# A causal attention block with a Fourier branch: float32r scores in array halves, and one static order with the stages beside the attention

## The reference

```
xn = layernorm(x)
q, k, v = xn @ wq, xn @ wk, xn @ wv        # q: 16 heads of 16, k and v: 4 heads of 16
q, k = rope(q), rope(k)
scores = einsum('bshd,bthd->bhst', q, k) / 4, causal mask
out = softmax(scores) @ v
y = real(ifft(einsum('bnd,do->bno', fft(xn), w))) + bias     # linear in xn: one 256 x 256 matrix
return x + out @ wo + y
```

## Time and profile before

| What | us |
|---|---|
| Median of 3 runs (1131.06 to 1132.2) | 1131.33 |
| Span of the profiled execution | 1130.0 |
| Busy PE, DVE, ACT, POOL | 1002.3, 866.3, 692.1, 184.0 |
| Opening and projections of batch 0 (0 to 121) | 121 |
| Attention of batch 0 (121 to 548) | 427 |
| Output block of batch 0, projections of batch 1 (548 to 693) | 145 |
| Attention of batch 1 (693 to 1100) | 407 |
| Output block of batch 1 | 30 |

### The profile page before, as it was taken

The page is one execution under the profiler, slowest core; times in us unless marked ns, Lnnn a source line. Parts: engine busy times, 40 slices in busy tenths (PEclk is TensorE's granted clock), DMA queues, the critical chain, the costliest instruction groups (busy, mean ns, idle before and its releaser), DMA issues. The chain is left out here.

```text
span 1130.0 us, 22198 instructions
## 1 busy us (share of the span) xinstructions
PE 1002.3 (89%) x6352; PEld 410.2 (36%) x6352; DVE 866.3 (77%) x1503; ACT 692.1 (61%) x1375; POOL 184.0 (16%) x241
## 2 busy tenths in 40 slices
PE   4975499999999999999888737999999999999998
PEld 3652233333333333322556423333333333333227
DVE  6796388889898888882449836888988988888706
ACT  1451256667677777779525413666767777777882
POOL 4680021010000000000028501211100000000000
PEclk9995699999999999999989758999999999999999
DMA  7099900000000000000014994000000000000002
GB/s 218 19 148 141 124 3 1 2 1 2 1 2 1 1 2 1 2 1 2 31 48 71 144 162 54 2 2 1 1 1 2 1 1 2 1 1 2 1 1 75
DMA packets 44527, 36.01 MB, mean 32 GB/s; under 512 B 11024, under 2 KB 44432, under 8 KB 44432
## 3 DMA queue, kind: packets, MB, share of 16 engines
q1 hardware_dynamic: 44432, 34.74, 17.8%
HBM read 21.89 MB, written 12.58 MB: 31 GB/s over the span
## 5 line engine op out<-in xcount | busy, mean ns | idle before, releaser
L456 ACT ACTIVATE share<-psS 128x512 f32<-128x512 f32 (+2 forms) x1104 | 568.5, 578 | 245.5 <-PE psS L858 240.2
L637 DVE TENSOR_REDUCE pmax<-psA 128x2 f32<-128x1024 f32 x384 | 456.4, 1220 | 54.2 <-PE psA L794 52.4
L794 PE MATMUL psA<-k_st,q_st 96*128 96x512 bf16 (+3 forms) x1280 | 354.5, 360 | 35.5 <-DVE pmax L625 14.7
L858 PE MATMUL psS<-q_st,k_st 98*128 98x512 bf16 (+3 forms) x1232 | 349.8, 350 | 35.3 <-DMA q_st<-spartT 34.0
L831 PE MATMUL psO<-share,v_sb 128*32 128x512 f32 (+3 forms) x2560 | 300.0, 541 | 6.3 <-ACT share L456 3.8
L371 POOL TENSOR_SCALAR_AFFINE_SELECT share<-share 128x512 f32<-128x512 f32 x128 | 81.2, 634 | 828.2 <-ACT share L456 828.2
L858 PEld LDWEIGHTS psS<-q_st,k_st 98*128 98x128 bf16 x1232 | 113.8, 97 | 265.7 <-ACT share L456 142.0
L794 PEld LDWEIGHTS psA<-k_st,q_st 96*128 96x128 bf16 x1280 | 110.3, 100 | 239.5 <-DVE pmax L637 77.4
L633 DVE CUSTOM_DVE_ANT_0 psA<-psA,mask 128x128 f32<-128x128 f32 (+3 forms) x256 | 119.0, 516 | 20.9 <-PE psA L794 20.9
L625 DVE TENSOR_REDUCE pmax<-psA 128x4 f32<-128x512 f32 (+2 forms) x96 | 98.9, 1042 | 22.8 <-PE psA L797 22.5
L831 PEld LDWEIGHTS psO<-share,v_sb 128*32 128x32 f32 x2560 | 50.4, 108 | 108.2 <-ACT share L456 55.3
(11 more groups left out here) (84 smaller groups left out, 631.4 us busy)
## 6 DMA issues: line engine op xcount, KB each, us to landing
q_st<-parts_scratch SPq DMA_DIRECT2D x48, 256.0 KB, 8.8
parts_scratch<-share SPq DMA_DIRECT2D x8, 1024.0 KB, 11.8
x_sb<-in_L_attn_x SPq DMA_DIRECT2D x8, 512.0 KB, 8.2
out<-x_sb SPq DMA_DIRECT2D x8, 512.0 KB, 3.0
k_st<-parts_scratch SPq DMA_DIRECT2D x48, 64.0 KB, 12.4
q_st<-spartT SPq DMA_DIRECT2D x128, 2.0 KB
share<-dft_tables SPq DMA_DIRECT2D x1, 512.0 KB, 4.1
share<-in_L_ffn_w_freq_real SPq DMA_DIRECT2D x1, 256.0 KB, 4.4
```

What stands on the lines that cost most here:

```text
L456: nc.scalar.activation(prob[:, u % 2, k * hp:(k + 1) * hp, s0:CH], score_bank(tail, bank)[:, 0:hp * w].rearrange("p (h s) -> p h s", h=hp) ...
L637: nc.vector.reduce_max(pmax[:, heads[0]:heads[0] + 2, i, q], psA[:, two:two + 2, :], AX.X).then_inc(S["a_reduced"], 1)
L794: last = mm(psA[:, 2 * (v % 2) + k // per, (k % per) * w:(k % per + 1) * w], q_st[0:ROWS, n, r, i * P:(i + 1) * P], k_st[0:ROWS, g, q * CH ...
L858: last = mm(score_bank(tail, bank)[:, h * w:(h + 1) * w], k_st[0:ROWS + SHIFT, g, tile * P:(tile + 1) * P], q_st[0:ROWS + SHIFT, nl, k * h ...
```

## The change

**Numbers.** Queries, keys and the shift are split into two float32r parts instead of three bf16 parts. A stack has 48 rows (three products of parts) and two rows for the shift. Two such stacks lie in one tile, in partitions 0 to 49 and 64 to 113, and hold the query heads r = 0, 1 and r = 2, 3. A score matmul therefore uses 64 rows of the array, and neighbouring matmuls go to opposite halves. The causal mask of the first pass is added on PE for all diagonal uses, by small bf16 matmuls in the same half; L633 is gone. The values product is as before, with 17 instead of 32 columns a head.

**One order.** `schedule()` walks through the whole kernel once when the kernel is built, with a duration for each job on each engine, and picks PE's next job by what is ready. It gives the orders of PE, ACT, POOL, DVE and SP, which are then written out. There is no stage for batch 1 and none for chunks 2 and 3 (chunk 1 is projected in the opening): transposes, projections and output tiles stand between the blocks of attention (`BESIDE` says how many by which step). The scores' ring of three banks is shared with these jobs.

**Rope.** Projections come out transposed, features on partitions, so no parts are transposed. Cosines and sines are spread over 128 partitions in the opening, by PE and ACT. POOL turns 20 of the 24 blocks (six operations of 512 columns each), DVE the first four. Queries are loaded by step (six DMAs for one key head), and kept for eight steps.

**Opening.** x comes in single tiles, statistics are made for four tiles at a time, DVE turns the first blocks, ACT and POOL fill constants and tables, and 30 small matmuls keep PE at work. x of batch 1 lies for its statistics in buffers that are used later.

```diff
-                w = (i + 1) * P if q == n // KV else CH
-                per = len(heads) // 2
...
-                pe.wait_ge(S["a_reduced"], b * ALL + v + 1)
-                for k, r in enumerate(heads):
-                    last = mm(psA[:, 2 * (v % 2) + k // per, (k % per) * w:(k % per + 1) * w], q_st[0:ROWS, n, r, i * P:(i + 1) * P],
-                              k_st[0:ROWS, g, q * CH:q * CH + w], start=True, stop=not on_pe(n, q))
...
+            def a_use(v, o):
...
+                two = slot_free(v)
+                bank = psA[:, two + o, :]
+                lo = (heads[o * per] // 2) * HALF
+                for k in range(per):
+                    last = mm(bank[:, k * w:(k + 1) * w], q_st[lo:lo + ROWS, n % (2 * KV), heads[o * per + k] % 2, i * P:(i + 1) * P],
+                              k_st[lo:lo + ROWS, slot_of(cc - j + q), g, 0:w], start=(k == 0), stop=q != j)
+                if q == j:
+                    for h in range(2):
...
+                        last = mm(to, mask_l[lo:lo + HALF, h, :], mask_r[lo:lo + HALF, h:h + 1, :].broadcast_to([HALF, per, HALF]), start=False, stop=h == 1)
...
+            def scores(g, k):
...
+                if u == 0 and k == 0:
+                    pe.wait_ge(shift_in[n % 2], 32 * CT * (n // 2 + 1))
+                bank = bank_of(("s", g, k))
+                for h in range(hp):
...
+                    lo = (r // 2) * HALF
+                    last = mm(bank[:, h * w:(h + 1) * w], k_st[lo:lo + FULL, key_slot(n, tile), kv, tile % CT * P:(tile % CT + 1) * P],
+                              q_st[lo:lo + FULL, n % (2 * KV), r % 2, s0:CH], start=True, stop=True)
...
+            def load_q(n, t):
...
+                if n >= 2 * KV:
+                    sp.wait_ge(S["pv_done"], BEGIN[n - 2 * KV + 1])
```

More of the change, by code:

```diff
@@ L36, in attention_fourier_block @@
+    STAGE_FIRST = (16, 17, 18, 19, 20)
+    LAG = 2
+    DEEP = 3
+    VW = HD + 1
+    GW = 32
     NEG = -1.0e30
+    WARM = (10, 20)
     EPS = 1e-5
[L38 to L46, removed]
+    QC0, KC0, VC0 = 0, D, D + P
+    WCOLS = D + P + KD
+    BY_HALF = (0, 2, 1, 3)
+    USES = (4, 4, 2, 2)
@@ L79, in attention_fourier_block @@
[L79 to L87, removed]
+        x_sb = sb("x_sb", [P, NJ * CT, D], fp32)
@@ L315, in _, with store @@
-            sp.wait_ge(S["out_stored"], NB * NJ * 16)
+            def store(m):
+                if m in FIRST:
+                    sp.wait_ge(S["first_parts"], 2 * FIRST.index(m) + 2)
+                else:
+                    sp.wait_ge(S["parts_done"], 2 * turned_by_pool(m) + 2)
+                cc = m // 3
+                w = KV if m % 3 == 0 else 2 * KV
+                at = D if m % 3 == 0 else (m % 3 - 1) * P
+                for half in range(2):
+                    for part in range(2):
+                        rows = scratch[cc, part, at:at + w * HD, :].rearrange("(h m n) s -> m h n s", m=2, n=N8)
+                        sp.dma_start(rows[half], parts[half * HALF:half * HALF + w * N8, m % 2, part, :].bitcast(fp32)).then_inc(stored[m % 2], 16)
@@ new lines, in _ @@
+            pool.wait_ge(S["rest_ready"], 5)
+            pool.wait_ge(S["first_parts"], 2 * len(FIRST))
+            before, masks, adds, biases = ("start",), 0, 0, 0
+            for job in POOL_ORDER:
+                if before[0] != "start" and (job[0] == "ones" or (job[0] == "r" and job[2] in (1, 2))):
+                    pool.wait_ge(*done_by(before, masks, adds, biases))
+                if job[0] == "mask":
+                    mask_diag(job[1])
+                    masks += 1
+                elif job[0] == "add":
+                    add_out(job[1], job[2], job[3])
+                    adds += 1
+                elif job[0] == "bias":
+                    add_bias(job[1])
+                    biases += 1
+                elif job[0] == "n":
+                    normalise(job[1])
+                elif job[0] == "ones":
+                    ones_rows(job[1], job[2])
+                else:
+                    rotate(job[1], job[2])
+                before = job
```

1870 lines of the change are left out of this document (1218 added, 652 removed).

## The result

The changed kernel takes 999.38 us (median of 4 runs), the kernel before beside it 1131.76: a ratio of 0.8816, with a 95% interval of 0.879 to 0.8842. The forecast was 845 us, with 812 to 925 as its range. The sign was right, the size was missed by 154 us. The ratio uses three of the four runs; the fourth, at a mean granted clock of 0.93 instead of 0.96 to 0.97, took 1025 us. The profiled run took 994.67 us, of which 993.0 are its span.

The account below looks back on a forecast made before the run. TensorE and VectorE were taken as bounds within 1%: through PE 56 + 742 - 6 + 14 = 806 us, through DVE 801. Waiting of 38 gave 844, and 1.3 carried over gave 845, range 812 to 925.

Parts of the forecast that it names:

- both rivals: Score matmuls: row halves bring no gain, 1015 to 1080 us, chance 0.08; float32r streams at fp32 rate, 1475 us, 0.04.
- changes of mode: TensorE switching between matmul types: 0.09 us each from the earlier trace; some hundred of them for the stages, 9 us.
- Two bf16 loads take 0.31: Stationary loads for score matmuls: two bf16 loads take 0.31 us, one load of 4-byte data 0.195.
- slower than before: Scores at fp32 rate, end 1475 us; slower once a 512-column score costs more than 0.24 us; chance 0.04.
- the bound engine before lost 3 to 5% in attention: Waiting between engines over the whole run: 5% taken, 38 us on 806, giving 844.
- In front of each step DVE is one or more steps ahead: Shift transfers before each attention step: costed at nothing inside the run and at 8 us at the end.
- an exponential that waits on a shift: Sign of being wrong: inside the run, an ACT exponential waiting on a shift transfer.
- No stretch at 1.2 GHz: Sign of being right: no stretch with the clock at 1.2 GHz between the first reduction and the end.
- supply: Late queries, shifts held in SyncE's queue or GpSimd slowing DVE's reductions: 35 to 80 us more, 880 to 925; chance 0.15.
- halves without gain: Score matmuls in opposite row halves save nothing, through waiting loads or taking turns: 1015 to 1080 us; chance 0.08.
- stages apart: Projection and output stages again stand apart from attention: otherwise idle DVE adds 100 us, 945; chance 0.02.

Follow-up runs that it names:

- one-half run: Changed kernel with every score matmul reading the first row half of the array: 1518 us in the median, from 1475 to 1629.
- bf16 runs: Changed kernel with score matmuls reading operands' upper two bytes as bf16, 944 us; and with operands split into two bf16 numbers instead of float32r, 940 us.
- whole, half and eighth work: Changed kernel (998 us) against maxima and exponentials both cut to the first half of their columns (937 us) or the first eighth (916 us).
- TensorE's savings: Changed kernel with values products of half their columns, from 936 to 981 us; and with mask matmuls left out, 991 us.
- an eighth of the work: Changed kernel with each maximum reading and each exponential writing only the first eighth of its columns, copied sums having 1000 added: 916 us.
- dummies: Changed kernel with two dummy fp32 matmuls of 128 columns after each first-pass use before the first second-pass score: 999.5 us.
- two-part bf16 version: Changed kernel with queries, keys and shifts split into two bf16 numbers instead of two float32r ones, order unchanged: 940 us.

## Why the prediction missed, step by step

**What held.** That two halves work at once (0.1175 a matmul against the 0.11 taken), and that float32r does not stream at the fp32 rate: both rivals fell, the first by the one-half run. By its rule that a load overlaps only where the row group differs, the Trainium skill's TensorE: Matmul & The Clock Gate (§ The mechanism) would have made the one-half order pay its loads; it took 0.235 a matmul where a load of 0.19 and 0.235 of columns would make 0.42, so the row holds again. The same section also lets a load go ahead of a matmul in flight into a background weight buffer, which would fit; no run here shows which it is. DVE has 696 us of work from 44.5 us on (731 less 35), 700 in the sum. A whole reduction has a mean of 1.220, as before, and those beside a two-input GpSimd operation (97) 1.221: no contention. Nor did queries run short: TensorE stood for their transfer once, 3.4 us. First reduction 44.9 for 48, last part 13.5 for 14. ACT 653 for 630. DVE was not over 85% busy, though: 74% (663.5 of 897.5 us in the long window), since it stands still for TensorE 110 us ahead of whole reductions alone.

**TensorE's terms.** Scores without changes of mode: 290 (361 less 71), in the sum 302. Values 280, in the sum 309 with 29 for changes of mode, so 280 without. Stages 130 for 122. Changes of mode: 71 (373 stretches of 0.19) for 38. This is the first mis-sized term, +33: the step took bf16's 0.09 from the earlier trace rows for a kind of load that the trace had at 0.195, and counted 320 + 100 changes, but not what the first load costs at each. The bf16 runs show its size. Two slips didn't enter the sum. "Two bf16 loads take 0.31" took the time from the first load's start to the second's end for their cost, where one takes 0.10. And slower than before would have begun at 0.27 us a 512-column score by the forecast's own terms (270 + 325 us over 1792 scores and 768 at half the price), not at 0.24.

**Waiting.** This is the step that failed: "the bound engine before lost 3 to 5% in attention", carried over as 38 us. The score stretches take 160 us over the floor, and at least 80 of it is waiting for DVE and ACT. The percentage came from busy shares, which cover short stops. Yet it was about right for the kernel before: read from starts, its score stretches in batch 1's attention take 262 us, some 20 over 0.09 a stretch and 0.217 for 512 columns (0.17, 0.11 and 0.06 for shorter ones), 5% of 407. The mistake was to carry it over to another balance. Before, DVE and ACT were busy for 328 and 295 us beside TensorE's 393 in batch 1's attention, 83 and 75% of it. Here the step's own sums (700 and about 630 beside 742) made it 94 and 85%, with three score banks and two slots between. That the waiting is for DVE and ACT is shown by the series of whole, half and eighth work; that the closeness of the sums is what made it grow is argued, and fits the 15 and 12 us of TensorE's savings that came back as waiting. The Trainium skill's TensorEngine Tiling (Array Packing) (§ PSUM Bottleneck) says that tiling speeds up TensorE but not the emptying of PSUM, which may then bind; the trace agrees, with 0.52 an exponential against 0.1175 a score matmul.

A smaller part is a term that was put at nothing: "In front of each step DVE is one or more steps ahead". In 14 of the 32 steps the first second-pass score comes only 6 to 10 us after DVE has made the shift (steps 4, 5, 7 to 13, 15 and 28 to 31, counted from 0), and the eight transfers take 5.2 to issue. At step 12 this shows as a stop of ACT:

```profile
362.00 0.21 DVE L1152 STREAM_TRANSPOSE spartT<-spart 128x32 f32<-128x32 f32 x1
...
362.24 5.22 SPq L719 DMA_DIRECT2D q_st<-spartT  x8
...
369.48 1.05 PE L1370 MATMUL psS<-q_st,k_st 50*128 50x512 f32 x3
...
370.20 0.60 ACT L986 ACTIVATE prob_sb<-psS 128x512 f32<-128x512 f32 x1 [10.50 <-PE psS L1370]
```

The stretch around it takes 12.6 us where the floor is 3.5, and with an eighth of the work still 9.9, part of it at 1.2 GHz in both. The prediction named this sign of being wrong, an exponential that waits on a shift. That it is the shift is argued from these times: the order also puts first-pass uses there, and DVE works 11.1 of the 12.6 us. What it cost over the whole run isn't divided from the rest.

**The opening.** First second-pass score at 66.9 for 56, +11: the first step's reductions end at 54.4, with 3 us of waiting for queries, and the order puts a second step's uses ahead of the first second-pass score.

**The clock.** "No stretch at 1.2 GHz" was wrong: 62 us in all (0.031 x 993 x 2), 37.5 of them from 44.4 to 82. They cost at most 31 us, and lie inside the items above, the 160 us over the floor among them.

**The balance.** Forecast span 844, measured 993. From 66.7 to 979.5 us the scores take 502: with the forecast's 6 us of them done earlier, 284 of columns (296 in the sum), 71 of changes of mode (38), 147 over the floor (where 38 of waiting stood). With stages (+8), values (0) and the opening (+11): -12 + 33 + 109 + 8 + 11 = 149. Of the 109, 42 is shown to be waiting (80 less the 38); the other 67 holds low clock, masks dearer than priced and waiting that no run took away, such as for shifts, and isn't divided between them. The rivals had no case for it: supply reached 880 to 925, halves without gain began at 1015, and 999 lay between, where no mechanism had been worked out. The case "stages apart" was right to be left at 0.02 but priced at 945, where the run gave 1317: the price took the stages' DVE time and left out the chain of hand-overs, first passes that run alone, and the clock.

## What to carry over

When a change speeds up the bound engine until two others come close to it (94 and 85% of its work here, 83 and 75% before), and they pass work through two or three buffers, take the wait at each hand-over from the timeline (one buffer's round trip against its share of the work), not as the old percentage. Read waiting on TensorE from starts of loads and matmuls, since "95% busy" held at least 80 us of it. And price a change of mode per stretch of equal work with the load of the new type in it: 4-byte operands cost 0.10 us at each of 373 stretches, 37 of the 58 us by which the two-part bf16 version of the same order is quicker.

## What the runs showed of the hardware that I had not expected

- TensorE at 1.2 GHz while busy all the time: 854 of 1514 us with scores in one half only (busy 99%), and from 45.5 to 93.3 us with dummies (46.97 of 47.50 us busy in the windows shown), all by recorded lengths. A busy share near 100% did not keep the clock up.
- Four score matmuls in row halves 1, 1, 0, 0 take the same 0.67 us as 1, 0, 0, 1, and the third then starts before the second.
- An exponential takes 0.26 us for 64 columns and 0.52 for 512, so cutting its columns by eight halves it only.
- A float32r stationary load takes 0.19 us, and with it short matmuls are dear: four of 128 columns take 0.22 beside two of 512, in bf16, with loads of 0.09, 0.12.
